# Fused cross attention and mixture of experts: all attention probabilities transposed by VectorE and regrouped through memory, with a fourth work bank

## The chip, the core and the metric

The kernel runs on one core of one Trainium2 chip. The metric is the device time of one execution in microseconds (us); lower is better. The core has five engines that work from their own instruction streams and meet at semaphores: TensorE (PE in the profile, its weight loads PEld), VectorE (DVE), ScalarE (ACT), GpSimd (POOL) and SyncE (SP, here the engine that issues nearly all DMA transfers).

## The reference

For 16 batches of 256 tokens of width 256, with a context of 256 tokens of width 192 for each batch:

```
q, k, v = layernorm(x) @ w_q, ctx @ w_k, ctx @ w_v        # 16 heads of 64
attn    = softmax(q @ k^T / 8)                            # per head, 256 x 256
x       = x + (attn @ v) @ w_o + b_o
g       = softmax(layernorm(x) @ router_w + router_b)     # 8 experts, top 2, capacity 640
x       = x + sum over the chosen experts of g * (gelu(h @ w1 + b1) @ w2 + b2)
```

## The kernel before

The kernel has two stages. The attention stage takes the first 700 us and is cut into 64 periods, four to a batch. Period m handles four heads (units 0 to 3) of 256 queries by 256 keys. The expert stage follows and is not touched by the change.

The order of the work is written out by hand. A function `timeline()` returns one list of (stage, number) pairs, and each engine walks that list and executes the stages that are its own. In period m (r is m modulo 4, the place in the batch) the engines do this:

- TensorE: `scores` of m (24 products into the PSUM banks 0 to 3, one bank a unit), `pv` of m-2 (probabilities times values), `q` and `k` of m+1 (projections), `v` of m, and between them the transposes `turn2` and `turn3` of m-1. In r=0 and r=2 comes a 24-product output projection `o`, in r=1 the transposes `xt` of the next batch, in r=2 and r=3 the router's `x2t` and `logits`.
- VectorE: four row maxima (`max0` to `max3`), `a_norm` of m-2 (the attended values times the inverse row sums, in place in PSUM), `inv`, `a_lo` of m-2, `q_lo`, `square0`, `k_lo`, `square1`, and then layer-norm and router work that differs with r.
- ScalarE: four exponentials `exp0` to `exp3` (two instructions each, with row sums), the copies `a_hi`, `q_hi`, `k_hi`, `v_sb` out of PSUM, and the copies of the two turned units (`copy2`, `copy3`).
- GpSimd: `ctx` (splits the next context), `ln1_root`, `ln2_root`, `residual`, and `scatter`, four indirect DMA writes a batch.
- SyncE: `inv_out` and `inv_in` (the inverse sums go through memory so that they come back spread over partitions), `lift` and `move`, and once a batch `traffic`.

The names with `_hi` and `_lo` are the two parts of a number: products of full precision are made of a rounded head and its remainder.

A probability tile must be transposed before it meets the values. That is done in two ways. In the 56 periods of `MOVED` (6 to 61), units 0 and 1 go through VectorE and memory: `square` transposes all 32x32 blocks in place, `lift` writes the tile to a table in memory, and `move` reads it back with the blocks in their turned places; `pv` two periods later uses it. Units 2 and 3 are transposed by TensorE into a PSUM bank (`turn`) and copied out by ScalarE. `by_pe(m)` says which units TensorE turns.

The results of `q`, `k`, `v`, `pv`, `xt`, `o`, `x2t` and `pos` share three PSUM banks (5 to 7) in rotation; each waits until the stage named in `WORK_READ` has read what was in the bank three works earlier. `logits` uses bank 4, which is the turns' bank.

Of the kernel before, what the change touches and what calls it, by code (L numbers as in the profile page):

```python
# [19 lines left out]
F32 = mybir.dt.float32  # L20
# [7 lines left out]
P = 128  # L28
B, S, D = 16, 256, 256
CD = 192  # L30
# [34 lines left out]
MOVED = range(6, PERIODS - 2)  # L65
SQ = 32
# [3 lines left out]
def by_pe(m):  # L70

    return (2, 3) if m in MOVED else (0, 1, 2, 3)

# [11 lines left out]
def timeline():  # L85
# [12 lines left out]
    for m in range(1, PERIODS - 2):  # L98
# [4 lines left out]
        out += [("scores", m)] + ([("pv", m - 2)] if m >= 2 else [])  # L103
        out += [("logits", b - 2)] if r == 3 and 2 <= b else []
# [16 lines left out]
        out += steps("exp0 exp1", m) + ([("a_hi", m - 2)] if m >= 2 else []) + [("q_hi", m + 1)]  # L121
        if four:
            out += [("copy0", m - 1), ("exp2", m), ("k_hi", m + 1), ("copy1", m - 1), ("exp3", m), ("copy2", m - 1),
                    ("v_sb", m)]
        else:
            out += [("copy2", m - 1), ("k_hi", m + 1), ("exp2", m), ("copy3", m - 1), ("exp3", m), ("v_sb", m)]
# [9 lines left out]
        out += ([("a_norm", m - 2)] if m >= 2 else []) + [("inv", m - 1)]  # L136
        out += [("slot", b - 3)] if r == 2 and 3 <= b else []
        out += [("bias", b - 2)] if r == 3 and 2 <= b else []
        out += [("ln1_stats", 1)] if m == 1 else []
        out += ([("a_lo", m - 2)] if m >= 2 else []) + [("q_lo", m + 1)]  # L140
        out += [("square0", m)] if m in MOVED else []
        out += [("k_lo", m + 1)]
        out += [("square1", m)] if m in MOVED else []
        if r == 0:
            out += steps("shift compare rank gate", b - 3) if 3 <= b else []
            out += [("ln1", b + 1)] if 1 <= b < B - 1 else []
# [3 lines left out]
        if r == 2:  # L150
# [11 lines left out]
                5: [("vsplit", 3)]}.get(m, [])  # L162
        out += [("scatter", b - 4)] if r == 0 and 4 <= b else []
# [5 lines left out]
        out += [("load_ctx", 3)] if m == 2 else []  # L169
        out += steps("inv_out inv_in", m - 1) + (steps("lift move", m) if m in MOVED else [])  # L170
# [1384 lines left out]
```

## Time and profile before

| | before |
|---|---|
| median of 3 runs | 955.09 us (954.37 to 957.1) |
| the profiled execution, own time | 957.82 us |
| its span, first to last instruction | 956.1 us |
| granted TensorE clock, mean | 0.992 of full |
| busy: PE | 918.1 us (96%) |
| busy: DVE | 739.8 us (77%) |
| busy: ACT | 573.8 us (60%) |
| busy: POOL | 280.2 us (29%) |

The span is the time from the first to the last instruction; the execution's own time is 1.7 us longer, and the median of the runs is 1.0 us below the span. Busy time is a sum of the stretches in which an engine has an instruction under way, so waits inside a stage do not count. The two stages have different limits, so the averages of the table say little about either.

### The profile page before, as it was taken

Reading aid. Unit: us, or ns where it says so; the run is one execution under the profiler, and the core shown is the slowest. Engines: PE = TensorE matmul, PEld = TensorE weight load, DVE = VectorE, ACT = ScalarE, POOL = GpSimd, SP = SyncE. Lnnn points to the kernel's source line nnn. Section 1 sums busy time; section 2 is a strip of 40 time slices with the busy share of each in tenths; the row PEclk is TensorE's granted clock in tenths of the full one; section 3 lists DMA queues with packets and bytes.
Section 4 is the critical chain, followed back from the end, with each engine's and each line's share of the span. In section 5 each row is a group of like instructions: output and inputs, shape, how many; then the busy total and the mean of one; then the engine's idle time right before and its main releaser. Section 6 shows DMA issues by size and latency. Waiting matters only on the chain.

```text
span 956.1 us, 22462 instructions
## 1 busy us (share of the span) xinstructions
PE 918.1 (96%) x7916; PEld 821.0 (86%) x7916; DVE 739.8 (77%) x1745; ACT 573.8 (60%) x1600; POOL 280.2 (29%) x441
## 2 busy tenths in 40 slices
PE   7999999999999999999999999999889999999995
PEld 7878888888888888888888888888689999999995
DVE  5757778888888888888888888877777877678762
ACT  5877766667667666766766677676534433334420
POOL 5541112314233231323223132302533223322233
PEclk9999999999999999999999999999899999999999
DMA  8462535445455445455444445444345765645422
GB/s 239 143 205 91 163 123 163 162 152 168 146 157 158 148 157 164 136 172 164 139 156 161 146 130 170 136 134 136 121 133 99 149 145 123 135 84 98 112 29 27
DMA packets 152991, 133.29 MB, mean 139 GB/s; under 512 B 62140, under 2 KB 141610, under 8 KB 152752
## 3 DMA queue, kind: packets, MB, share of 16 engines
q1 hardware_dynamic: 144048, 122.87, 42.9%
q0 software_dynamic: 8832, 8.98, 5.4%
q8 instruction: 64, 1.05, 0.5%
q14 instruction: 47, 0.39, 0.1%
HBM read 82.15 MB, written 54.61 MB: 143 GB/s over the span
## 4 chain that ended last, share of the span: by engine, by line
PE 70%; DVE 11%; ACT 10%; issue 4%; DMA 3%; POOL 0%; SPq 0%; POOLq 0%; ACTq 0%; DVEq 0%
PE psum L734 20%; PE psum L839 9%; PE psum L996 9%; PE psum L855 9%; PE psum L980 8%; PE psum L801 7%; ACT prob L1067 6%; PE psum L819 5%; DVE negmax L1255 3%; DVE hidl L1201 2%; DVE bufl L1201 1%; ACT probt L1007 1%; DVE hidh L1488 1%; PE psum L879 1%; DVE psum L1274 1%
## 5 line engine op out<-in xcount | busy, mean ns | idle before, releaser
L1067 ACT ACTIVATE prob<-psum,negmax 128x256 f32<-128x256 f32 x512 | 238.0, 481 | 79.5 <-DVE negmax L1255 79.4
L1255 DVE TENSOR_REDUCE negmax<-psum 128x2 f32<-128x512 f32 x256 | 160.4, 682 | 29.7 <-PE psum L801 29.7
L1173 ACT ACTIVATE hid<-psum,b1t 128x640 f32<-128x640 f32 x64 | 50.9, 795 | 126.6 <-PE psum L980 125.0
L839 PE MATMUL psum<-probt,v 128*64 128x256 f32 x1024 | 124.6, 385 | 0.0
L707 POOL DMA_INDIRECT out_rows<-y,rowi x40 | 66.3, 1658 | 160.8 <-DVE y L1498 154.2
L1067 ACT ACTIVATION_READ_ACCUMULATOR prob<-psum,negmax 128x1 f32 x512 | 109.5, 214 | 0.0
L839 PEld LDWEIGHTS psum<-probt,v 128*64 128x64 f32 x1024 | 67.8, 136 | 36.4 <-issue 0.3
L668 POOL DMA_INDIRECT slot_table<-row,picki x64 | 66.8, 1044 | 96.9 <-PE psum L734 61.2
L996 PE MATMUL psum<-w2h,hidh 128*128 128x256 f32 x320 | 91.4, 286 | 2.9 <-DVE y L1498 1.5
L801 PE MATMUL psum<-kh,qh 64*128 64x256 f32 x512 | 82.5, 316 | 11.1 <-ACT prob L1067 8.9
L996 PE MATMUL psum<-w2l,hidh 128*128 128x256 f32 x320 | 90.5, 283 | 0.0
L996 PE MATMUL psum<-w2h,hidl 128*128 128x256 f32 x320 | 90.5, 283 | 0.0
L1007 ACT ACTIVATE probt<-psum 128x512 f32<-128x512 f32 x144 | 87.3, 609 | 4.4 <-PE psum L819 4.4
L819 PE MATMUL psum<-ident,prob 128*128 128x128 f32 x576 | 87.1, 276 | 2.7 <-ACT prob L1067 2.7
L734 PE MATMUL psum<-xth,wqh 128*128 128x256 f32 x256 | 78.9, 308 | 0.5 <-DVE xtl L1201 0.5
L1279 DVE STREAM_TRANSPOSE prob<-prob 128x512 f32<-128x512 f32 x112 | 78.6, 702 | 0.0
L855 PE MATMUL psum<-woh,ah 128*128 128x256 f32 x256 | 72.9, 285 | 1.6 <-DVE al L1201 1.6
L606 POOL TENSOR_SCALAR shifted<-ln_mean_var 128x2 f32<-128x2 f32 x32 | 7.1, 223 | 225.0 <-issue 182.7
L801 PE MATMUL psum<-kl,qh 64*128 64x256 f32 x512 | 72.9, 278 | 0.0
L801 PEld LDWEIGHTS psum<-kh,qh 64*128 64x128 f32 x512 | 48.8, 185 | 27.9 <-ACT prob L1067 13.3
L801 PE MATMUL psum<-kh,ql 64*128 64x256 f32 x512 | 72.8, 277 | 0.0
L855 PE MATMUL psum<-wol,ah 128*128 128x256 f32 x256 | 72.4, 283 | 0.0
(199 smaller groups left out, 2704.6 us busy)
## 6 DMA issues: line engine op xcount, KB each, us to landing
squares<-prob SPq DMA_DIRECT2D x56, 512.0 KB
probt<-squares SPq DMA_DIRECT2D x224, 128.0 KB, 2.8
invrows<-inverses SPq DMA_DIRECT2D x128, 128.0 KB
w1r<-in_w SPq DMA_DIRECT2D x8, 1024.0 KB
w2r<-in_w SPq DMA_DIRECT2D x8, 1024.0 KB, 9.1
slot_table<-blank SPq DMA_DIRECT2D x8, 662.5 KB, 6.5
blocks<-slot_table SPq DMA_DIRECT2D x56, 80.0 KB
xin<-in_x SPq DMA_DIRECT2D x16, 256.0 KB, 3.5
```

Source lines behind the costliest of these rows:

```text
L668: pool.indirect_dma_start(out=table, out_offset=bass.IndirectOffsetOnAxis(ap=picki[:, b % 3, k, t:t + 1], axis=0), in_=row[:, b % 3, t, :] ...
L734: mm = pe.matmul(dst, lhs, rhs, start=(j == 0), stop=(j == len(terms) - 1))
L801: mm = pe.matmul(psum[:, 2 * cc + h, qb * S:(qb + 1) * S], a[r, m % 2, cc, cols], w[r, m % 2, cc, :], start=(j == 0), stop=(j == len(terms ...
L819: mm = pe.transpose(psum[:, TURN_BANK[u], kb * S + qb * P:kb * S + (qb + 1) * P], prob[:, m % 2, u, kb, qb, :], ident[:, :])
L839: mm = pe.matmul(dst[h * HD:(h + 1) * HD, cc * S:(cc + 1) * S], v[:, b % 2, kb, cols], p, start=(kb == 0), stop=(kb == ST - 1))
L855: mm = pe.matmul(dst[:, 0:D], a[:, b % 2, c, tt], w[:, c, :], start=(c == 0 and j == 0), stop=(c == PAIRS - 1 and j == 2))
L980: mm = pe.matmul(dst, lhs, rhs, start=(n == 0), stop=(n == len(terms) - 1))
L996: mm = pe.matmul(dst, a[:, j, ss], w[:, j, :], start=(j == 0 and m == 0), stop=(j == HC - 1 and m == 2))
L1007: copy = lambda dst, src, **kw: act.activation(dst, src, ACT.Copy, **kw)
L1067: last = act.activation(into, out_of, ACT.Exp, bias=negmax[:, m % 2, u, qb:qb + 1], accum_out=total[:, m % 2, u, qb:qb + 1])
L1255: dve.tensor_reduce(negmax[:, m % 2, u, :], psum[:, u, :].rearrange("p (q s) -> p q s", q=ST), AX.X, ALU.max, negate=True).then_inc(sem("m ...
L1279: dve.transpose(at, at).then_inc(sem("square"), 1)
```

## The change

All four units of a moved period now go through VectorE and memory, and TensorE turns none of them. Seven things change with that:

1. `turn2`, `turn3`, `copy2` and `copy3` are gone from the 56 periods. The layout of the moved tile covers four units: `square` handles two units in an instruction, `lift` and `move` carry twice the bytes in as many transfers, and `pv` reads all its probabilities in the moved layout.
2. `exp` of m waits for `lifted` of m-2 and no longer for `moved`.
3. TensorE's order in a period becomes `scores`, `logits` (in r=3), `q`, `k`, `pv`, `v`. ScalarE's becomes `exp0 exp1 q_hi exp2 k_hi exp3 a_hi v_sb`. VectorE's becomes `max0..3 inv q_lo square0 k_lo a_norm square1`.
4. Bank 4 joins the rotation of work banks (`places()`), and `logits` uses that rotation.
5. `a_norm` writes a new tile `attended` in SBUF, which frees its bank; `a_hi` reads that tile.
6. `a_lo` of the periods 4 to 59 and `ln1` of the batches from 2 on move from VectorE to GpSimd. `attended` is one tile, so `a_norm` of m waits for `a_lo` of m-1.
7. The context's raw tiles `c0` and `c1` have one buffer in place of two, `scatter` waits for `k` and no longer for `q`, and SyncE issues `lift` between `inv_out` and `inv_in`.

The core of the diff:

```diff
 def by_pe(m):
-    return (2, 3) if m in MOVED else (0, 1, 2, 3)
+    return () if m in MOVED else (0, 1, 2, 3)
...
         if four:
+            out += [("scores", m)] + ([("pv", m - 2)] if m >= 2 else [])
             out += [("q", m + 1), ("turn0", m - 1), ("k", m + 1), ("turn1", m - 1), ("v", m), ("turn2", m - 1)]
         else:
-            out += [("q", m + 1), ("turn2", m - 1), ("k", m + 1), ("turn3", m - 1), ("v", m)]
+            out += [("scores", m)] + ([("logits", b - 2)] if r == 3 and 2 <= b else [])
+            out += [("q", m + 1), ("k", m + 1), ("pv", m - 2), ("v", m)]
...
+        out += [("inv_out", m - 1)] + ([("lift", m)] if m in MOVED else [])
+        out += [("inv_in", m - 1)] + ([("move", m)] if m in MOVED else [])
...
-WORK_READ = {"xt": "xt_lo", "q": "q_lo", "k": "k_lo", "v": "v_sb", "pv": "a_lo", "o": "x2", "x2t": "x2t_sb",
+WORK_READ = {"xt": "xt_lo", "q": "q_lo", "k": "k_lo", "v": "v_sb", "pv": "a_norm", "o": "x2", "x2t": "x2t_sb",
...
+def places():
...
+    banks, last, found = [5, 6, 7], {}, {}
+    for stage, n in TIMELINE:
...
+        if work in WORKS and work not in found:
+            at = banks.pop(0)
+            banks.append(at)
+            found[work] = at, last.get(at)
+            last[at] = work
+        if (stage, n) == ("turn3", MOVED[0] - 1):
+            banks.append(4)
...
-                sp.dma_start(square_table[m % 2], prob_pair(m)).then_inc(sem("lifted"), 16)
+                sp.dma_start(square_table[m % 2], prob_all(m)).then_inc(sem("lifted"), 16)
...
-                at = work_bank("pv", m).rearrange("p (c s) -> p c s", c=2)
-                dve.tensor_tensor(at, at, invrows[:, :, :], ALU.mult).then_inc(sem("a_norm"), 1)
-
-            def square(m, u):
-                dve.wait_ge(sem("exp"), UNITS * m + u + 1)
-                at = prob_pair(m).rearrange("p (g u c) -> p u g c", g=GROUPS, u=2)[:, u]
+                if m >= 1:
+                    dve.wait_ge(sem("a_lo"), m)
+                dve.tensor_tensor(attended[:, :, :], work_bank("pv", m).rearrange("p (c s) -> p c s", c=2),
+                                  invrows[:, :, :], ALU.mult).then_inc(sem("a_norm"), 1)
+
+            def square(m, pair):
+
+                dve.wait_ge(sem("exp"), UNITS * m + 2 * pair + 2)
+                at = prob_all(m).rearrange("p (g v c) -> p v g c", g=GROUPS, v=2)[:, pair]
                 dve.transpose(at, at).then_inc(sem("square"), 1)
...
+            def a_lo(m):
+                b, c = divmod(2 * m, PAIRS)
+                pool.wait_ge(sem("a_hi"), m + 1)
```

VectorE in a period with r=3 of a middle batch, before: `al` is `a_lo`, `ql` and `kl` are `q_lo` and `k_lo`, and the two transposes of `prob` are `square0` and `square1`.

```order
L1255 TENSOR_REDUCE negmax<-psum 128x2 x4
L1274 TENSOR_TENSOR psum<-psum,invrows 128x512
L1264 RECIPROCAL invtot<-total 128x8
L1267 STREAM_TRANSPOSE invturned<-invtot 128x32
L1334 TENSOR_TENSOR logit<-psum,rb_all 128x16
L1201 TENSOR_TENSOR al<-psum,ah 128x512
L1244 SCALAR_TENSOR_TENSOR ql<-psum,qh 128x512
L1279 STREAM_TRANSPOSE prob<-prob 128x4x128
L1201 TENSOR_TENSOR kl<-psum,kh 128x512
L1279 STREAM_TRANSPOSE prob<-prob 128x4x128
```

The same period of the changed kernel:

```order
L1303 TENSOR_REDUCE negmax<-psum 128x2 x4
L1312 RECIPROCAL invtot<-total 128x8
L1315 STREAM_TRANSPOSE invturned<-invtot 128x32
L1384 TENSOR_TENSOR logit<-psum,rb_all 128x16
L1292 SCALAR_TENSOR_TENSOR ql<-psum,qh 128x512
L1330 STREAM_TRANSPOSE prob<-prob 128x4x256
L1249 TENSOR_TENSOR kl<-psum,kh 128x512
L1323 TENSOR_TENSOR attended<-psum,invrows 128x512
L1330 STREAM_TRANSPOSE prob<-prob 128x4x256
```

The transposes have doubled in width, `al` is gone, and the product with the inverse sums has moved from second place to just before the last transpose.

GpSimd in r=0 and r=1 of a middle batch, before: the context's split, the four scatters, the residual's bias, and the first instruction of `ln2_root`.

```order
L593 TENSOR_TENSOR c1s<-c,c1t 64x256
L594 TENSOR_TENSOR c0l<-c,c0h 128x256
L668 DMA slot_table<-row,picki 5120x265 x4
L631 TENSOR_TENSOR xin<-xin,bo_all 128x256 x2
L606 TENSOR_SCALAR shifted<-ln_mean_var 128x2
```

The same place of the changed kernel:

```order
L619 TENSOR_TENSOR c1s<-c,c1t 64x256
L620 TENSOR_TENSOR c0l<-c,c0h 128x256
L644 TENSOR_SCALAR turning<-xin,ln_mean_var,ln_rstd 128x256 x2
L713 DMA slot_table<-row,picki 5120x265 x4
L676 TENSOR_TENSOR xin<-xin,bo_all 128x256 x2
L655 TENSOR_TENSOR al<-attended,ah 128x512
L632 TENSOR_SCALAR shifted<-ln_mean_var 128x2
```

`ln1` stands ahead of the scatters and `a_lo` behind the residual, so this `a_lo` also waits for what those two wait for.

SyncE in r=1 and at the start of r=2 of a middle batch, before; the four transfers between the moves and the next `inverses` are `traffic` (the last row of it is two):

```order
L466 DMA inverses<-invturned 4x32x32
L475 DMA invrows<-inverses 64x2x256 x2
L485 DMA squares<-prob 128x1024
L492 DMA probt<-squares 32x4x256 x4
L404 DMA xin<-in_x 128x2x256
L500 DMA out_rows<-x 128x2x256
L411 DMA c<-in_ctxt 128x256
L413 DMA c<-in_ctxt 64x256 x2
L466 DMA inverses<-invturned 4x32x32
L475 DMA invrows<-inverses 64x2x256 x2
L485 DMA squares<-prob 128x1024
```

The same place of the changed kernel:

```order
L492 DMA inverses<-invturned 4x32x32
L511 DMA squares<-prob 128x2048
L501 DMA invrows<-inverses 64x2x256 x2
L518 DMA probt<-squares 32x4x512 x4
L433 DMA xin<-in_x 128x2x256
L526 DMA out_rows<-x 128x2x256
L440 DMA c<-in_ctxt 128x256
L442 DMA c<-in_ctxt 64x256 x2
L492 DMA inverses<-invturned 4x32x32
L511 DMA squares<-prob 128x2048
L501 DMA invrows<-inverses 64x2x256 x2
```

The lift to `squares` has doubled and stands ahead of the reload of the inverse sums.

## Rows read from the trace of the kernel before

**Rows 1.** Windows of two batches: length, then PE, PEld, DVE, ACT, POOL busy

```profile
215.59:257.63 42.04, 41.30 (x380) 35.57 (x379) 35.35 (x93) 29.12 (x92) 11.70 (x23) 1.00 0.52 160
425.79:467.83 42.04, 41.30 (x380) 35.57 (x379) 35.35 (x93) 29.11 (x93) 11.68 (x23) 1.00 0.48 155
```

**Rows 2.** Waits in the second batch: us in total, times, longest

```profile
DVE negmax L1255 <- PE psum L801: 1.2, 2, 0.9
...
DVE x L1297 <- PE psum L855: 0.3, 1, 0.3
...
PE psum L734 <- DVE valid L1382: 0.3, 1, 0.3
```

**Rows 3.** Chain of work in r=0 and r=1: start, us, what

```profile
430.10 1.64 PE psum L734 x12
431.74 0.44 PE psum L819 x4
432.18 1.19 PE psum L734 x10
...
437.82 1.62 PE psum L801 x24
439.44 1.88 PE psum L839 x16
```

**Rows 4.** Timeline of PE across one turn: start, us, engine, line

```profile
431.57 0.60 PE L819 MATMUL psum<-ident,prob 128*128 128x128 f32 x4
431.93 0.36 PE L734 MATMUL psum<-c0h,wkh 128*128 128x256 f32 x1
```

**Rows 5.** Groups of instructions by form: busy us, mean ns, idle before

```profile
L1279 DVE STREAM_TRANSPOSE prob<-prob 128x512 f32<-128x512 f32 x112 | 78.6, 702 | 0.0
...
L1201 DVE TENSOR_TENSOR al<-psum,ah 128x512 fp32r<-128x512 f32 x64 | 44.2, 691 | 19.1 <-ACT ah L1007 19.1
...
L1470 DVE STREAM_TRANSPOSE turned<-blocks 128x640 f32<-128x640 f32 x14 | 11.6, 834 | 0.0
...
L631 POOL TENSOR_TENSOR xin<-xin,bo_all 128x256 f32<-128x256 f32 x32 | 23.4, 730 | 52.9 <-DMA slot_table<-row,picki 30.2 <-DVE turning L1217 21.1 <-POOL ln_rstd L611 0.3
...
L622 POOL TENSOR_TENSOR w1l<-w1r,w1h 128x1024 fp32r<-128x1024 f32 x2 | 4.8, 2407 | 3.9 <-DMA slot_table<-row,picki 3.9
```

**Rows 6.** Timeline of DVE: r=3 ends, r=0 begins; `ln1` in r=0

```profile
425.53 0.70 DVE L1279 STREAM_TRANSPOSE prob<-prob 128x512 f32<-128x512 f32 x1
426.15 0.13 DVE L1431 TENSOR_REDUCE pick<-lowkey 128x2 f32<-128x16 f32 x1
...
427.30 2.47 DVE L1255 TENSOR_REDUCE negmax<-psum 128x2 f32<-128x512 f32 x4
...
437.74 0.74 DVE L1217 TENSOR_SCALAR turning<-xin,ln_mean_var,ln_rstd 128x256 f32<-128x256 f32 x2
```

**Rows 7.** Timeline of SP's DMA queue: start, us to issue, line, transfer

```profile
436.61 0.54 SPq L485 DMA_DIRECT2D squares<-prob  x1
440.34 1.82 SPq L492 DMA_DIRECT2D probt<-squares  x4
...
449.37 1.73 SPq L492 DMA_DIRECT2D probt<-squares  x4
...
453.87 0.58 SPq L466 DMA_DIRECT2D inverses<-invturned  x1
456.55 1.27 SPq L475 DMA_DIRECT2D invrows<-inverses  x2
```

**Rows 8.** The page's DMA issues: count, KB each, median us to landing

```profile
probt<-squares SPq DMA_DIRECT2D x224, 128.0 KB, 2.8
```

**Rows 9.** Timeline of POOL in r=0

```profile
426.02 0.39 POOL L590 CAST c1s<-c 64x256 fp32r<-64x256 f32 x1 [8.03 <-PE psum L734]
...
432.62 1.09 POOL L668 DMA_INDIRECT slot_table<-row,picki  x1 [3.63 <-PE psum L734]
...
440.59 1.54 POOL L631 TENSOR_TENSOR xin<-xin,bo_all 128x256 f32<-128x256 f32 x2 [2.95 <-DMA slot_table<-row,picki]
```

More of the change, by code:

```diff
@@ L118, in timeline @@
         out += [("pos", b - 3)] if r == 1 and 3 <= b else []
-        out += steps("exp0 exp1", m) + ([("a_hi", m - 2)] if m >= 2 else []) + [("q_hi", m + 1)]
         if four:
+            out += steps("exp0 exp1", m) + ([("a_hi", m - 2)] if m >= 2 else []) + [("q_hi", m + 1)]
             out += [("copy0", m - 1), ("exp2", m), ("k_hi", m + 1), ("copy1", m - 1), ("exp3", m), ("copy2", m - 1),
@@ L125, in timeline @@
         else:
-            out += [("copy2", m - 1), ("k_hi", m + 1), ("exp2", m), ("copy3", m - 1), ("exp3", m), ("v_sb", m)]
+            out += [*steps("exp0 exp1", m), ("q_hi", m + 1), ("exp2", m), ("k_hi", m + 1), ("exp3", m),
+                    ("a_hi", m - 2), ("v_sb", m)]
         if r == (1 if b else 2) and b + 1 < B:
@@ L135, in timeline @@
         out += ([("split_lo", 5)] if m == 1 else []) + steps("max2 max3", m)
[L136 to L142, printed above, removed]
+        if four:
+            out += ([("a_norm", m - 2)] if m >= 2 else []) + [("inv", m - 1)]
+            out += [("ln1_stats", 1)] if m == 1 else []
+            out += ([("a_lo", m - 2)] if 0 <= m - 2 < POOL_REST[0] else []) + [("q_lo", m + 1)]
+            out += [("square0", m)] if m in MOVED else []
+            out += [("k_lo", m + 1)]
+        else:
+            out += [("inv", m - 1)] + ([("slot", b - 3)] if r == 2 and 3 <= b else [])
+            out += [("bias", b - 2)] if r == 3 and 2 <= b else []
+            out += [("q_lo", m + 1), ("square0", m), ("k_lo", m + 1), ("a_norm", m - 2)]
         out += [("square1", m)] if m in MOVED else []
@@ L162, in timeline @@
                 5: [("vsplit", 3)]}.get(m, [])
+        out += [("ln1", b + 1)] if r == 0 and 1 <= b < B - 1 else []
         out += [("scatter", b - 4)] if r == 0 and 4 <= b else []
@@ L189, in timeline @@
             ("gelu_table", 0)]
-    out += [*steps("max0 max1 max2 max3", m), ("inv", m - 1), ("slot", c - 1), ("a_norm", m - 2), ("q_lo", z),
-            ("a_lo", m - 2), ("k_lo", z), ("ln2", c), *steps("keys pick", c - 1), ("x2add", ST * d), ("inv", m),
+    out += [*steps("max0 max1 max2 max3", m), ("inv", m - 1), ("slot", c - 1), ("q_lo", z), ("k_lo", z),
+            ("a_norm", m - 2), ("a_lo", m - 2), ("ln2", c), *steps("keys pick", c - 1), ("x2add", ST * d), ("inv", m),
             *steps("max0 max1 max2 max3", z), ("a_norm", m - 1), ("a_lo", m - 1), *steps("bias shift", c),
@@ L685, in _ @@
                     inverse_root(stage[:3], n)
+                if stage == "ln1" and n >= 2:
+                    ln1(n)
+                if stage == "a_lo" and n in POOL_REST:
+                    a_lo(n)
                 if stage == "vsplit":
@@ L844, in o @@
                 b, t = divmod(n, ST)
[L845 removed]
+                dst = bank("o", n) if chunks[0] == 0 else psum[:, PLACES["o", n][0], :]
                 tt = slice(t * P, (t + 1) * P)
@@ L1453, in _ @@
             for stage, n in TIMELINE:
-                if stage in steps:
+                if stage in steps and not (stage == "ln1" and n >= 2) and not (stage == "a_lo" and n in POOL_REST):
                     steps[stage](n)
```

127 lines of the change are left out of this document (70 added, 57 removed).

## The prediction

> **What bounds the kernel now.** I read the windows first. Two batches 210 us apart take 42.04 us each with the same busy times [rows 1], so the attention stage is a fixed cycle of one batch, four periods, and one batch can be priced and multiplied. In it PE is busy for 41.30 us, all but 0.74; the next column but one, DVE, has 35.35, ACT 29.1. The last columns say that the granted clock is full and that the 16 DMA engines are busy for about half of the time. So TensorE's own work sets the time of this stage. The waits say how far the second engine is from that. DVE has seven entries in the batch, from 1.2 us down to 0.3, in sum 5.8 us [rows 2]. What it does not wait is its own: 42.04 - 5.8 = 36.2 us, which is its 35.35 busy plus 0.9 of short gaps between instructions that depend on each other. The chain of work then confirms the bound: from r=0 into r=1 it runs through PE's steps one after another, 1.64 for `q`, 0.44 for a turn, 1.19 for `k`, later 1.62 for `scores` and 1.88 for `pv` [rows 3].
>
> **What the change takes from TensorE.** Eight turns a batch. The chain gives one 0.44 us [rows 3]. Start to start in the timeline it is 0.36 (431.57 to 431.93) [rows 4]; the rest is the slower first product behind it, which a change of operand may cost anyhow. I take the middle, 0.40. The 56 moved periods are 14 batches, so 112 turns x 0.40 = 44.8 us, with 40.3 and 49.3 as its ends. Besides, PE idles 0.74 us a batch. One of these waits is for `valid`, the reader of the `pos` bank, 0.3 us [rows 2]; with a fourth bank, and that reader now ahead of `q_lo`, it should go. I give half of the idle time back: 14 x 0.37 = 5.2 us. The sum is 50 us, with everything else hidden.
>
> **What it puts on VectorE.** Each of the two transposes grows from 512 to 1024 elements. The trace has 702 ns for 512 and 834 for 640, 1.03 ns an element [rows 5], so 1024 takes 1.23 us, 0.53 more. Per period that is +1.06. `a_lo` leaves: 0.69 of duration, but consecutive instructions of this kind start 0.62 apart (425.53 to 426.15) [rows 6], so -0.62. `ln1` leaves: 0.74 once a batch [rows 6]. The batch becomes 36.2 + 4 x 1.06 - 4 x 0.62 - 0.74 = 37.2 us. TensorE's becomes 42.04 - 3.2 - 0.4 = 38.4. So VectorE ends 1.2 us a batch under the new bound, 97% occupied, and its present 5.8 us of waits must shrink to 1.2. This is the step that I trust least. For it speaks the new order. Counted from the start of `scores`, the first bank is full at about 1.0; four maxima take 2.47 [rows 6], `inv` 0.4, and `q_lo` can start near 3.9. ScalarE has made two units and `q_hi` by about 4.1. Then come `square0` to 5.9, `k_lo` to 6.5, `a_norm`, whose `pv` ends at 1.62 + 1.64 + 1.19 + 1.88 = 6.3 [rows 3], and `square1` at 7.1, when `exp3` has ended near 6.5. Each product stands just behind its releaser, and `a_norm` no longer has `a_hi` and `a_lo` directly behind it. Batch work that is uneven over r (2.5 us of router work in r=0 where PE has an `o` of 24 products, little in r=3 where PE has none) falls in the same periods on both engines, so the lag between them stays within a microsecond. `exp3` must be done only when the second half of the next `scores` begins, some 3 us later; this is the play between the two.
>
> **ScalarE** loses two copies a period and was no bound. `a_hi` now reads SBUF, which may cost some tens of ns on an engine with 13 us of idle time a batch: nothing.
>
> **The trip through memory.** Lift before: issued at 436.61, its data landed when `move` is issued at 440.34: 3.7 us for 512 KB [rows 7]. The moves took 1.82 to issue and 2.8 to land [rows 7, 8], some 4.6. If size cost nothing the trip stays 8.3 us; if all doubles it is 16.6. Between these ends I take, as an estimate, that half of each step grows with the bytes: 12.5 us. `square1` ends about 8.3 us after its period's `scores`; `pv` stands two periods later, behind `scores`, `q` and `k` (4.45). With a period of 9.6 us the trip may take 2 x 9.6 + 4.45 - 8.3 = 15.3 us. So it is hidden with 2.8 us to spare, and in the worst case late by 1.3.
>
> SyncE's queue is the tighter place. In r=1 it issues the moves at 449.37 and, behind `traffic`, the next `inverses` only at 453.87 and the reload `invrows` at 456.55 [rows 7]. After the change the lift stands ahead of that reload and takes 1 to 2 us more, so the reload lands about 8 to 9 us behind `square1` of r=2. Its reader is `a_norm` in the next period (r=3), about 8 us behind that `square1`: a wait of 0 to 1 us, once a batch.
>
> **GpSimd.** `a_lo` is 512 elements wide: 730 ns for 256 and 2407 for 1024 give 2.18 ns an element [rows 5], so 1.29 us. In r=0 it stands behind the scatters. The first scatter started 0.9 us behind the end of `q` and now follows `k`, 1.19 later; the four take until 5.0 us later, the residual waited 2.95 more and took 1.54 [rows 3, 9]. From the start of r=0: 1.62 + 1.64 + 1.19 + 0.9 + 5.0 + 2.95 + 1.54 + 1.3 = 16.1 us. r=0 lasts about 10.5, so `attended` comes free 5.6 us into r=1, and `a_norm` there wants it at about 6.5. It holds by 0.9 us. A scatter that lands 2 us later on busier DMA engines costs VectorE 1 us a batch. These two places are why I give back only half of PE's idle time.
>
> There is a price that could sink the change: GpSimd now reads and writes SBUF for 1.3 us more a period. In the trace a 512-wide transpose (425.53 to 426.23) has a GpSimd cast from SBUF starting at 426.02 inside it; both keep their usual 702 and 390 ns [rows 5, 6, 9]. So I price this contention at nothing; the other end is that VectorE stands still for each `a_lo`, 1.29 us a period. The Trainium skill speaks against the change here. Its page "SBUF — State Buffer", section "SBUF: two separate sides", says that VectorE and GpSimd share a port pair as an exclusive lock, which a VectorE operation in a two-port mode or with two SBUF inputs takes for its whole length. Read strictly it covers here the router's comparisons and the layer norm, not the transposes, if these run in one-port mode; by that rule the sum moves by a microsecond or two at most.
>
> **Sum.** Profiled: span 956.1 - 50 = 906, own time 957.8 - 50 = 908. The median of the runs shown is 2.7 us under that profiled execution, so 905.
>
> **Rivals.**
>
> *VectorE takes over.* For it: two engines near 97% in a loop rarely both run free, and VectorE waits seven times a batch even now, with 14% of its time to spare. Against it: the order above. If half of the 5.8 us stays, the batch is 37.2 + 2.9 = 40.1 us, and the gain 14 x 1.9 = 27: 928. If all stays, 43.0 and 14 us slower. Chance of something between 913 and 952: 0.22.
>
> *GpSimd blocks VectorE* (ends slower). If every `a_lo` stops VectorE for 1.29 us, VectorE's batch is 37.2 + 5.2 = 42.4 and with 1.2 us of waits 43.6: 955 + 14 x 1.5 = 977. It decides from about 0.9 us of blocking a period on. Against it stands the overlap above: 0.05. The skill's rule, were the transposes two-port operations, is this case.
>
> *The trip is late.* It becomes slower than before only when the trip exceeds 2 x 10.5 + 4.45 - 8.3 = 17.2 us, above even the doubled 16.6. At 16.6 the period settles where 2p - 3.85 = 16.6, p = 10.2: gain 14 x 1.2 = 17, 938. Chance 0.05.
>
> *It saves more.* Turns at 0.44 and all of PE's idle time gone: 49.3 + 10.4 = 60 us, 895. Chance of under 897: 0.08.
>
> **How the numbers follow.** The forecast, TensorE still the bound and 897 to 913, has 0.58; what is left, 0.02, is the change doing nothing. The range for 8 in 10 leaves out the low case and the slow end: 896 to 930 takes all of the forecast and most of the first rival. About 0.3% (3 us) is what a measurement of this kernel can tell from no change; faster by more 0.91, within it 0.03, slower 0.06 (the blocking case and the far end of the first rival).
>
> **What would show it.** Right: a batch of 38 to 38.8 us; PE busy for over 97% of it with no `ident,prob` products; VectorE near 96%; transposes of 1.23 us; GpSimd's `al` near 1.29. The rivals would show as `scores` waiting for `prob` while DVE is full, as transposes longer than 1.3 us while GpSimd works, as `pv` waiting for the DMA of `squares`, or as `attended` waiting for `al` (r=1) or `invrows` (r=3).

## The result and the profile after

| | before | after |
|---|---|---|
| median | 955.42 us (954.37 to 957.1, 4 runs) | 985.12 us (982.63 to 987.04, 4 runs) |
| span of the profiled execution | 956.1 us | 980.9 us |
| mean granted clock | 0.992 | 0.983 |

The ratio is 1.031, 95% interval 1.028 to 1.034. The forecast was 905 us. The changed kernel is 30 us slower than before, 80 from the forecast. Further down, one run each of e16 (1001.25 us) and e19 (952.10 us) was slow, over 1.5% above the fastest of its kernel, and the medians given here leave it out.

First the page of the changed kernel: section 1, the DMA rows of section 2 (40 slices, each digit the busy share in tenths), the chain, and the issues with their time to landing.

```profile
PE 887.5 (90%) x7468; PEld 780.1 (80%) x7468; DVE 749.3 (76%) x1661; ACT 513.0 (52%) x1488; POOL 386.9 (39%) x525
...
DMA  8465888888887888888879887887543855545422
GB/s 232 134 207 172 241 259 232 243 241 260 238 242 230 232 257 247 226 243 261 238 225 251 253 241 230 234 258 210 161 148 78 168 127 128 108 79 129 110 28 27
...
DMA 28%; PE 24%; POOL 17%; DVE 12%; issue 11%; ACT 4%; SPq 4%; POOLq 0%; DVEq 0%; ACTq 0%
...
squares<-prob SPq DMA_DIRECT2D x56, 1024.0 KB, 6.1
probt<-squares SPq DMA_DIRECT2D x224, 256.0 KB, 5.0
...
xin<-in_x SPq DMA_DIRECT2D x16, 256.0 KB, 6.1
```

The chain that ended last runs for 28% of the span through transfers, more than through TensorE. PE has lost 30.6 us of work (918.1 to 887.5), and yet the span grew by 24.8. A move that landed 2.8 us after its issue [rows 8] now takes 5.0. The load of `xin`, which the change does not touch, takes 6.1.

Two windows, the steady stretch and one batch, with columns as in [rows 1]. The last two are the busy share of the DMA engines and GB/s.

```profile
127.39:653.03 525.64, 469.60 (x4125) 391.29 (x4122) 431.20 (x1021) 296.72 (x997) 224.94 (x339) 0.99 0.84 242
394.08:437.62 43.54, 38.82 (x349) 32.56 (x345) 35.99 (x87) 24.71 (x84) 19.23 (x29) 1.00 0.87 245
```

The batch takes 43.54 us where 38 to 38.8 was forecast, and 42.04 before. PE's work is 38.82 us, down from 41.30 (the prediction's terms give 41.30 - 3.2 = 38.1), so the turns are saved. But 4.7 us of the batch are now idle on PE. The busy share of the DMA engines, 0.52 and 0.48 in the two batches of [rows 1], is 0.87. VectorE has 35.99 us of work, and its waits in this batch fill nearly all of the rest, 36.0 + 7.2 = 43.2 of 43.54:

```profile
DVE stats L1256 <- DMA xin<-in_x: 3.6, 1, 3.6
DVE attended L1323 <- POOL al L655: 2.5, 1, 2.5
DVE ql L1292 <- ACT qh L1054: 1.1, 4, 0.3
```

Two places hold VectorE for 6.1 us in this batch. Both stand behind transfers. First r=2, on SyncE's queue and on VectorE's timeline:

```profile
424.55 1.73 SPq L518 DMA_DIRECT2D probt<-squares  x4
426.69 0.40 SPq L433 DMA_DIRECT2D xin<-in_x  x1
...
432.46 0.76 DVE L1256 BATCH_NORM_STATS2 stats<-xin 128x6 f32<-128x256 f32 x2 [3.60 <-DMA xin<-in_x]
```

The load goes out directly behind 1 MB of moves and takes 5.8 us, while VectorE stands in front of it with everything else of r=2 queued behind. Then r=0 on GpSimd (compare [rows 9]), and what VectorE waits for in r=1:

```profile
445.68 2.44 POOL L644 TENSOR_SCALAR turning<-xin,ln_mean_var,ln_rstd 128x256 f32<-128x256 f32 x2
448.30 1.12 POOL L713 DMA_INDIRECT slot_table<-row,picki  x1 [0.18 <-POOL turning L644]
...
457.86 1.54 POOL L676 TENSOR_TENSOR xin<-xin,bo_all 128x256 f32<-128x256 f32 x2 [4.54 <-DMA slot_table<-row,picki]
459.49 1.28 POOL L655 TENSOR_TENSOR al<-attended,ah 128x512 fp32r<-128x512 f32 x1
...
460.89 0.69 DVE L1323 TENSOR_TENSOR attended<-psum,invrows 128x512 f32<-128x512 f32 x1 [1.25 <-POOL al L655]
```

`ln1` (2.44 us) stands ahead of the scatters, the residual waits 4.54 us for them in place of 2.95, and the remainder ends at 460.8. VectorE's wait for it is 1.25 us here and 2.5 in the batch above.

### The profile page after: what moved, and what is told of

The parts are those of the page before. It is cut to its first block, busy times and chain, and to the rows that moved or that the text cites. A ratio compares the mean times of both kernels' runs of the same rounds, so it can differ in the third digit from the quotient of the medians.

```text
span 980.9 us, 21255 instructions
## 1 busy us (share of the span) xinstructions
PE 887.5 (90%) x7468; PEld 780.1 (80%) x7468; DVE 749.3 (76%) x1661; ACT 513.0 (52%) x1488; POOL 386.9 (39%) x525
## 4 chain that ended last, share of the span: by engine, by line
DMA 28%; PE 24%; POOL 17%; DVE 12%; issue 11%; ACT 4%; SPq 4%; POOLq 0%; DVEq 0%; ACTq 0%
DMA squares<-prob 9%; PE psum L1043 9%; PE psum L1027 8%; DMA xin<-in_x 7%; DMA slot_table<-row,picki 7%; POOL al L655 4%; POOL slot_table L713 4%; SPq L518 3%; DVE prob L1330 3%; DMA inverses<-invturned 2%; PE psum L779 2%; POOL turning L644 2%; POOL xin L676 2%; ACT prob L1115 2%; DVE hidl L1249 2%
## 5 line engine op out<-in xcount | busy, mean ns | idle before, releaser
L1115 ACT ACTIVATE prob<-psum,negmax 128x256 f32<-128x256 f32 x512 | 241.3, 492 | 161.6 <-DVE negmax L1303 157.2
L886 PE MATMUL psum<-probt,v 128*64 128x256 f32 x1024 | 129.4, 396 | 12.6 <-DMA probt<-squares 12.4
L1330 DVE STREAM_TRANSPOSE prob<-prob 128x1024 f32<-128x1024 f32 x112 | 137.9, 1232 | 0.7 <-ACT prob L1115 0.7
L1115 ACT ACTIVATION_READ_ACCUMULATOR prob<-psum,negmax 128x1 f32 x512 | 114.8, 224 | 0.0
L886 PEld LDWEIGHTS psum<-probt,v 128*64 128x64 f32 x1024 | 74.2, 141 | 48.8 <-issue 21.3
L655 POOL TENSOR_TENSOR al<-attended,ah 128x512 fp32r<-128x512 f32 x56 | 71.6, 1279 | 72.6 <-ACT ah L1054 69.4
L846 PE MATMUL psum<-kh,qh 64*128 64x256 f32 x512 | 80.4, 304 | 11.6 <-issue 7.2
L1054 ACT ACTIVATE ah<-attended 128x512 fp32r<-128x512 f32 x64 | 40.5, 633 | 87.2 <-DVE attended L1323 87.2
L1323 DVE TENSOR_TENSOR attended<-psum,invrows 128x512 f32<-128x512 f32 x64 | 43.6, 682 | 40.4 <-POOL al L655 28.2
```

The lines of the kernel that those rows point to most:

```text
L655: pool.tensor_tensor(al[:, b % 2, c:c + 2, :], attended[:, :, :], ah[:, b % 2, c:c + 2, :].bitcast(F32), ALU.subtract).then_inc(sem("a_lo" ...
L846: mm = pe.matmul(psum[:, 2 * cc + h, qb * S:(qb + 1) * S], a[r, m % 2, cc, cols], w[r, m % 2, cc, :], start=(j == 0), stop=(j == len(terms ...
L886: mm = pe.matmul(dst[h * HD:(h + 1) * HD, cc * S:(cc + 1) * S], v[:, b % 2, kb, cols], p, start=(kb == 0), stop=(kb == ST - 1))
L1115: last = act.activation(into, out_of, ACT.Exp, bias=negmax[:, m % 2, u, qb:qb + 1], accum_out=total[:, m % 2, u, qb:qb + 1])
L1330: dve.transpose(at, at).then_inc(sem("square"), 1)
```

## The experiments

Medians over 3 rounds each (5 for e18 and e19), against runs of the kernel before on the same chip, which gave 955.9 (e1 to e4), 956.4 (e6 to e9), 958.8 (e10 to e12), 958.7 (e13 to e16) and 958.1 (e17 to e19). There is no e5. The stretch 130 to 600 us is used for windows and waits unless another is named.

The expectations name their theories by letters. A: the doubled traffic makes transfers late, and two of them stop VectorE. B: the new order of the stages and VectorE's load set the time. C: GpSimd blocks VectorE. D: SyncE's queue, which issues and waits one step after another, sets the time. E: the rate of the 16 DMA engines sets it. H: a move that writes 32 partitions is slow and the order of such moves matters. W: the scattered write into SBUF is slow, and not the 32 partitions.

**Are the two waits the loss?** e1 moves the statistics of the layer norm and their root from r=2 to r=3, e2 puts GpSimd's remainder ahead of the residual in r=0, e3 does both.

```diff
-            out += [("ln1_stats", b + 2)] if b + 2 < B else []
+        out += [("ln1_stats", b + 2)] if r == 3 and b + 2 < B else []
...
+        out += [("a_lo", m - 2)] if r == 0 and m - 2 in POOL_REST else []
         out += [("residual", b + 1)] if r == 0 and 1 <= b < B - 1 else []
```

> The changed kernel with one edit: the first layer norm's statistics of batch b+2 and their root are moved from r=2 to the end of r=3, some 10 us behind the load that they read. In the changed kernel VectorE waits 3.6 to 4.9 us a batch there for the transfer of xin. Theory A (the doubled traffic makes single transfers late, and two of them stop VectorE): this wait goes and the batch falls by 2.5 to 4 us over some 13 batches, so 985 becomes 935 to 952; the wait of attended for al in r=1 stays at about 2.3 us a batch. Rival B (the new order of the steps and VectorE's load set the time, and the wait only fills slack): the time that VectorE waited for xin comes back as other waits, result 975 to 988. Rival C (GpSimd blocks VectorE through the shared memory port): no change beyond 5 us.

> The changed kernel with one edit: in r=0 GpSimd's a_lo stands between the scatters and the residual, so it no longer waits for the scatters' transfers to land. Theory A: the 2.3 us a batch that attended waits for al in r=1 go; since r=1 leads to the late load in r=2, whose time is set by SyncE's queue and not by VectorE, part of it comes back there: 955 to 975. Rival B: 980 to 988. Rival C (port): no change.

> Both edits together. Theory A: both waits go, the batch comes to 38.5 to 40 us, and the kernel to 915 to 930, below the kernel before (955). Rival B: it stays above 955. Rival C: GpSimd's blocking stays in, so 945 or more, with transposes and scalar operations of VectorE longer than in the kernel before while al runs.

Measured: e1 987.29 (ratio 1.032, 1.030 to 1.034), e2 988.32 (1.034, 1.033 to 1.036), e3 980.21 (1.026, 1.024 to 1.028). Each cured wait is gone from its trace and comes back elsewhere. In e1 `attended` waits 35.9 us for `al` where the changed kernel has 26.5 in the same stretch; in e2 the wait for `xin` is 45.1 where it was 39.2. With both gone, 5 of the 80 us are back, where theory A expected 915 to 930. So the two waits are not the loss; they are where VectorE met it first. Theories B and C still stand after these three runs. In e3 it is PE that waits for the moves (8.6 us in this stretch of the changed kernel):

```profile
PE psum L887 <- DMA probt<-squares: 30.9, 17, 3.0
```

SyncE's own queue waits in e3 (127 to 653 us, as engine line waited for: total, times, longest):

```profile
SPq L502 <- DMA inverses<-invturned: 169.5, 48, 4.7
SPq L519 <- DMA squares<-prob: 73.4, 49, 2.8
```

So a 16 KB transfer that was handed over right behind 1 MB of moves holds SyncE's queue 3.5 us a period.

**The bytes.** e4 lifts and moves only the first half of each block row (the other half of the probabilities that `pv` reads is old). e8 lifts all and moves half.

```diff
-                sp.dma_start(square_table[m % 2], prob_all(m)).then_inc(sem("lifted"), 16)
+                sp.dma_start(square_table[m % 2].rearrange("p (g c) -> p g c", g=GROUPS),
+                             prob_all(m).rearrange("p (g c) -> p g c", g=GROUPS)[:, :, 0:256]).then_inc(sem("lifted"), 16)
```

> The changed kernel, with lift and move carrying half of each tile (256 of every 512 columns, 512 KB a step as in the kernel before); the attention output is built in part from old probabilities. Instructions and order on the five engines are those of the changed kernel. Theory A: DMA share falls from 0.85 to about 0.5 and the transfers land about as before, xin's wait falls below 1 us and al's below 0.5 us a batch: 905 to 925, near what was predicted. Rivals B and C: the bytes don't matter, 970 to 988.

> The changed kernel with only the moves cut to half the bytes (256 of every 512 columns; the rest of a tile keeps what it had, so the attention output is not the reference's); the lift carries all 1024 KB. With both halved the kernel takes 911. Moves fill the DMA engines for 4 to 5 us a period at 235 GB/s, the lift for 2.6 at 400. Theory E: most of the loss is with the moves, 920 to 935. Theory D: the loop loses only the moves' part ahead of inverses, and a similar 915 to 940. If the lift's size was the cost, 955 to 980.

Measured: e4 911.26 (0.953, 0.952 to 0.955), e8 922.67 (0.965, 0.962 to 0.968). With the bytes of before, all other parts of the change give what was forecast, to within 6.3 us, which rules out B and C as the main cause: order, engines and GpSimd's work are those of the changed kernel. Of the 74 us between e4 and the changed kernel, 62 go with the second half of the moves and then 11 with that of the lift. The two windows (e4, then e8) have 165 and 216 GB/s:

```profile
130.00:600.00 470.00, 463.31 (x4178) 388.88 (x4177) 436.61 (x1036) 302.37 (x1010) 226.79 (x337) 1.00 0.56 165
```

```profile
130.00:600.00 470.00, 454.99 (x4101) 381.57 (x4101) 427.25 (x1017) 294.31 (x989) 222.68 (x334) 1.00 0.65 216
```

One batch of e4 has TensorE busy from end to end, in 38.8 us as forecast; the eleven loads of `xin` in the stretch are 38.8 us apart in the mean too:

```profile
413.50:452.30 38.80, 38.80 (x353) 32.62 (x353) 36.70 (x90) 25.67 (x86) 19.79 (x30) 1.00 0.56 169
```

A kernel with the lift alone halved was not tried.

**Traffic without the change.** e9 is the kernel before with two copies of 512 KB from the table to spare memory behind the moves of each period.

```diff
+                for h in range(2):
+                    sp.dma_start(spare[m % 2, h], square_table[m % 2]).then_inc(sem(f"moved{m % 2}"), 16)
```

> The kernel before, unchanged in its order and its engines' work, with two more copies of 512 KB from memory to memory behind each period's four moves (from the table of squares to a spare table), which pv and the next exponentials wait for with the moves. That is as much added traffic as the change adds. If the traffic alone costs the time (theories D and E), the kernel before slows down too: 985 to 1040, with VectorE waiting for xin or PE for the moves. If the loss needs the change's order of steps on the engines (theory B), it stays within 955 to 965.

Measured 1125.54 (1.176, 1.170 to 1.181), the worst miss of the expectations. The copies share the moves' counter, so `pv` waits for them too (58.7 us in the stretch), and the granted clock of the stretch fell from 1.00 to 0.93; the size is not a price of traffic alone. What can be read are the waits for transfers that the edit did not touch. Before, this stretch had 2.5 us of waits for `invrows` and 1.1 for `xin`:

```profile
DVE psum L1277 <- DMA invrows<-inverses: 71.9, 28, 4.6
DVE stats L1211 <- DMA xin<-in_x: 40.5, 9, 6.2
```

**SyncE's order.** e6 is e3 with the move of m-1 ahead of `inv_in`, and the lift behind it, so that no wait for `inverses` holds the lift. e7 is e6 with the four moves issued for partition groups 0, 2, 1, 3.

```diff
-        out += [("inv_out", m - 1)] + ([("lift", m)] if m in MOVED else [])
-        out += [("inv_in", m - 1)] + ([("move", m)] if m in MOVED else [])
+        out += [("inv_out", m - 1)] + ([("move", m - 1)] if m - 1 in MOVED else [])
+        out += [("inv_in", m - 1)] + ([("lift", m)] if m in MOVED else [])
...
-                for g in range(GROUPS):
+                for g in (0, 2, 1, 3):
```

> Both edits of the third experiment, and SyncE's order changed: a period now issues inv_out of m-1, move of m-1, inv_in of m-1, lift of m, traffic. So the small write of the inverse sums no longer queues behind the four moves, and its reload no longer behind a lift. In the third experiment SyncE spent 3.5 us a period waiting for the landing of inverses and 1.5 for the lift, one after the other, in a loop of about 10 us. Theory D (the serial loop of SyncE's queue sets the period, not the bytes): the wait for inverses goes, the loop has slack, the batch comes to 38 to 39.5 us and the kernel to 905 to 930. Theory E (the 16 DMA engines' bandwidth sets the period; they are busy for 86% and each transfer only waits for others): the DMA share rises to above 0.93 at most, the batch falls by no more than 3 us of 43, 945 to 975.

> The kernel e6_order, with the four moves issued for the partition groups 0, 2, 1, 3 in place of 0, 1, 2, 3. Each move writes 32 of 128 partitions and the trace shows 16 busy DMA engines moving only about 235 GB/s while moves run, against 400 or more in a lift. If neighbouring moves share a part of the memory's ports, alternating halves raises the rate of the moves and takes 5 to 20 us from e6_order under theory E, less than 5 under theory D. If the rate comes from reading 2 KB pieces, no change within 3 us.

Measured: e6 990.13 (1.035, 1.033 to 1.038), e7 975.68 (1.021, 1.018 to 1.024). In e6 the wait for `inverses` is gone (2.3 us where e3 has it at every period) but the moves go out later, `pv` waits 45.2 us for them, and the kernel is 10 us slower than e3. Both expectations missed (D 905 to 930, E 945 to 975). This order of the queue gains nothing; that a part of the loss is SyncE's serial order is not ruled out by it. e7 gained 14.5 us with nothing but the order of four equal DMAs, within the 5 to 20 expected.

**The shape of the DMAs.** All on the base of e3, all with the same bytes. e10 is e3 with the order 0, 2, 1, 3. e11 issues groups 0 and 1 from SyncE and 2 and 3 from ScalarE. e12 lets the lift do the regrouping, so that the move is one DMA over 128 partitions. e13 and e14 leave the regrouping out (`pv` reads probabilities in the wrong places): one move of 128 partitions, and four moves of 32 in which each partition takes one run of 8 KB. A tile of 1 MB over 128 partitions is 8 KB in each, so a regrouping move takes four runs of 2 KB; the expectations of e13 and e14 have both at half their size.

```diff
e12
-                sp.dma_start(square_table[m % 2], prob_all(m)).then_inc(sem("lifted"), 16)
+                for a in (0, 2, 1, 3):
+                    sp.dma_start(square_table[m % 2].rearrange("(g j) (a c) -> a j g c", a=GROUPS, g=GROUPS)[a],
+                                 prob_all(m)[a * SQ:(a + 1) * SQ, :].rearrange("j (g c) -> j g c", g=GROUPS))\
+                      .then_inc(sem("lifted"), 16)
...
e12 and e13, in place of the four moves
+                sp.dma_start(probt_all(m), square_table[m % 2]).then_inc(sem(f"moved{m % 2}"), 16)
e14
+                    sp.dma_start(probt_all(m)[g * SQ:(g + 1) * SQ, :], square_table[m % 2][g * SQ:(g + 1) * SQ, :])\
```

> e3 (both waits cured) with one thing changed: the four moves of a period are issued for partition groups 0, 2, 1, 3 in place of 0, 1, 2, 3. Same bytes, same number of DMAs, same order of everything else. Theory H (a move of 32 partitions reaches only some of the ports of SBUF, and neighbouring groups share them, so that the order decides how well two moves in flight overlap): some 10 to 16 us below e3's 980, as the same edit brought 14.5 us on another base, so 964 to 970, with a higher rate of the DMA engines. Rival (bytes alone set the period, and the gain on the other base was one of order): 977 to 983.

> e3 with moves of groups 0 and 1 issued from SyncE's queue and those of groups 2 and 3 from ScalarE's queue, so that both halves are written at the same time and SyncE issues two DMAs a period less. Theory H: as e10 or better, 955 to 970. Rival that the queue of SyncE is the bound (its issues one behind another): better than e10 too, with SyncE's wait for the inverses gone. Rival that bytes alone set the period: 977 to 983. If ScalarE's wait for the lift holds up its exponentials: above 985, with ScalarE waiting for the DMA of squares.

> e3 with the regrouping done on the way out: four lifts of 32 partitions each write the table in the layout of the destination, and one move of 1 MB over all 128 partitions brings it back. Same bytes, same number of DMAs a period. Theory H (a DMA over 32 partitions is the slow part, wherever it stands): the lift becomes slow, the move fast; the sum changes little, 970 to 985, unless writes into SBUF are slower than reads from it. Theory W (it is the scattered write into SBUF that is slow, not the 32 partitions): 925 to 955, the DMA share down towards 0.7.

> e3 with the regrouping left out altogether: one lift of 1 MB and one move of 1 MB, both over 128 partitions and in one piece of 4 KB a partition, so that the value products read probabilities in the wrong places; the bytes are the same as in e3, a period has two DMAs less than e12's five. Theory W/H (the shape of the DMAs costs, not the bytes): at or below e12's 945, 915 to 935, the DMA share at 0.75 or lower, since e4 with half of the bytes took 911. Rival (bytes alone): 970 to 980.

> e3 with four moves over 32 partitions each as there, but each partition takes one run of 4 KB in place of four of 1 KB (again no regrouping, the value products read probabilities in the wrong places). If the 32 partitions are what slows a move, it stays near e3: 970 to 985. If the runs of 1 KB do it, it comes near e13: 915 to 940.

| | move | us | less the kernel before | ratio | DMA share | GB/s |
|---|---|---|---|---|---|---|
| e3 | 4 x 32 partitions, 2 KB runs | 980.21 | +24.3 | 1.024 to 1.028 | 0.86 | 245 |
| e10 | the same, order 0, 2, 1, 3 | 969.64 | +10.8 | 1.007 to 1.013 | 0.84 | 248 |
| e14 | 4 x 32 partitions, 8 KB runs | 958.04 | -0.7 | 0.997 to 1.002 | 0.88 | 254 |
| e11 | as e3, from two queues | 956.51 | -2.3 | 0.995 to 1.001 | 0.84 | 255 |
| e12 | 1 x 128, the lift regroups | 945.10 | -13.7 | 0.982 to 0.993 | 0.82 | 262 |
| e13 | 1 x 128, no regrouping | 932.91 | -25.8 | 0.971 to 0.976 | 0.78 | 267 |

The windows of e3, e14 and e13 in this order:

```profile
130.00:600.00 470.00, 423.62 (x3700) 355.76 (x3696) 395.15 (x929) 267.75 (x894) 207.05 (x315) 0.97 0.86 245
```

```profile
130.00:600.00 470.00, 435.12 (x3851) 364.19 (x3852) 407.79 (x957) 279.32 (x933) 212.78 (x328) 0.99 0.88 254
```

```profile
130.00:600.00 470.00, 452.64 (x4071) 378.17 (x4070) 428.80 (x1011) 295.42 (x980) 225.59 (x342) 1.00 0.78 267
```

e13 moves more bytes a second at a lower busy share than e3. The busy share counts the time that the engines hold a packet, not what they carry.

The kernel before ran 3 us slower beside e10 to e14 than beside e3, so the differences to it are the safer measure. By them the 50 us between e3 and e13 (47 in the times) split into 25 (22) for the runs of 2 KB in place of 8 KB (e3 to e14) and 25 for four DMAs of 32 partitions in place of one of 128 (e14 to e13). e14 fell between its two expectations for that reason: both things cost. The second step changes two things at once, the partitions that a DMA reaches and the number of DMAs, which these runs do not part.

e10 shows that the order matters by itself (13.5 us), since it changes neither the number nor the bytes. e12 bears out W rather than H alone: its four lifts are of 32 partitions and in runs of 2 KB too, and yet it is 38 us faster than e3. But the shape acts on SyncE's queue as well: its wait for `inverses`, 151.8 us in e3 in this stretch, is 40.7 in e13 and 3.4 in e12. And the bytes themselves cost: e13, of the cheapest shape, is still about 20 us above e4.

The Trainium skill, page "SBUF — State Buffer", section "Door 1: The DMA port swizzle (why [64,N] ≈ [32,N])", says that partitions 0 to 63 are reached through one half of the 16 DMA ports and 64 to 127 through the other, so that groups 0 and 1 use the same half and 2 and 3 the other. The gains of e7 and e10 fit that mapping, but no trace here shows a port, so it is a reading and not a shown cause. e11 does not decide it: two queues also halve the time in which SyncE issues moves (1.73 us for four in the changed kernel), though SyncE still waits 123.4 us for `inverses` there.

**The order of the stages, with the cheaper shape.** e15 is the changed kernel with e12's lift and move and neither stage of e3 moved; e16 has the statistics moved, e17 the remainder. e18 is e15 with the remainder of one period in four, the one due in r=0, back on VectorE behind `square1`; e19 is e18 with the statistics in r=3.

```diff
+def on_pool(m):
+    return m in POOL_REST and m % PER_B != 2
...
+        out += [("a_lo", m - 2)] if m - 2 in POOL_REST and not on_pool(m - 2) else []
```

> The changed kernel with the regrouping done by the lift, as e12, but without e3's two moves of stages. With less trouble in the DMA engines the two moves of stages may be worth nothing: e12's trace has VectorE's row operation (128 x 256) at 0.75 us against 0.42 elsewhere, since GpSimd's al now runs beside it. 935 to 945 if that costs more than the waits they cure; 950 to 960 if the waits for xin and al come back.

> e15 with only the statistics of the layer norm moved to r=3 (the load of xin gets one more period). If e15 waits for xin: 5 to 15 us better than e15, 930 to 942. If not: within 3 us of it.

> e15 (the lift regroups) with only GpSimd's remainder put ahead of the residual in r=0. e15 waits 31 us for xin and 10 for al, e12 with both moves of stages takes 945, e16 with the statistics alone 990. If the late remainder is what e16 shows (al waits 48 us there) and the wait for xin is worth some 20 to 30 us by itself, this run keeps the wait for xin and loses the one for al: 945 to 955. If curing one of the two waits always feeds the other, as with e1 and e2: above 960.

> e15 with the remainder of the period that ends in r=0 back on VectorE, behind square1: GpSimd's queue behind the scatters then holds none of the remainders, at 0.62 us a batch for VectorE. If the lateness of that remainder is what is left of the loss: 930 to 945, with VectorE's waits for al gone, those for xin staying (some 30 us in 470). Rival (VectorE is now the bound, at 90% busy): 950 to 960.

> e18 with the statistics of the layer norm in r=3 as well, so that neither the load of xin nor a remainder stands behind a late transfer. If these two waits and the shape of the moves were the whole of the loss beside the bytes: at or below e12's 945, 925 to 940, near e13's 933. If the waits return elsewhere, as in e16: above 960.

Measured: e15 955.33 (0.995 to 0.998), e16 988.84 (1.026 to 1.031), e17 957.18 (0.998 to 1.001), e18 948.64 (0.987 to 0.993), e19 939.69 (0.978 to 0.983). e17 fell between its two expectations, and so did e18, in which the waits for `al` are gone and those for `xin` stay at 30.2 us. e16 is the miss to learn from: with the wait for `xin` cured alone it is 34 us slower than e15. GpSimd's queue gets the root of the layer norm in r=3, where it waits for VectorE's statistics, and holds a remainder and all of r=0's work behind it (GpSimd's timeline in e16):

```profile
441.83 0.23 POOL L632 TENSOR_SCALAR shifted<-ln_mean_var 128x2 f32<-128x2 f32 x1 [12.08 <-DVE ln_mean_var L1259]
...
444.03 1.28 POOL L655 TENSOR_TENSOR al<-attended,ah 128x512 fp32r<-128x512 f32 x1
```

In r=1 the late remainder then holds VectorE, and VectorE holds TensorE (e16's waits):

```profile
DVE attended L1323 <- POOL al L655: 48.2, 10, 7.6
...
PE psum L779 <- DVE attended L1323: 34.7, 10, 6.4
```

With r=0's remainder out of GpSimd's queue the same edit gains 9 us (e18 to e19). e19 is 2.0% faster than the kernel before (0.980, 0.978 to 0.983), the best that computes the whole. Its window, and the longest waits left of DVE, PE and ACT's exponentials:

```profile
130.00:600.00 470.00, 447.16 (x3973) 373.85 (x3972) 426.97 (x999) 287.52 (x955) 205.63 (x322) 0.99 0.82 260
```

```profile
DVE ql L1300 <- ACT qh L1062: 17.5, 35, 2.8
...
PE psum L926 <- DVE row L1273: 17.2, 11, 2.6
...
ACT prob L1123 <- DMA squares<-prob: 48.8, 19, 3.0
```

PE and VectorE hardly wait for a transfer any more, but ScalarE does: `exp` waits for the lift that empties its tile, 48.8 us in the stretch, the longest of these waits, and VectorE's wait for `qh` stands behind ScalarE. A third buffer for `prob` was not tried.

**TensorE's clock.** A part of the loss that the waits do not name is the granted clock. In the changed kernel PE is busy for 0.09 of the 2 us from 300 to 302, and from 304 to 306 it works at 0.50, the lower of its two levels (1.2 of 2.4 GHz), with 12 products done where 27 are done from 308 to 310:

```profile
300.00:302.00 2.00, 0.09 (x2) 0.07 (x1) 1.90 (x12) 0.00 (x0) 0.95 (x2) 1.00 0.79 321
...
304.00:306.00 2.00, 2.00 (x12) 1.11 (x10) 1.68 (x6) 2.00 (x8) 0.39 (x1) 0.50 0.66 155
```

Added up over slices of 5 us of the stretch, the clock that was not granted comes to 0 us in the kernel before, e4, e8 and e13, to 5.1 in the changed kernel, 3.4 in e14 and e15, 12.0 in e3, 17.4 in e16 and 20.4 in e6 (in the profiled execution of each). As an estimate, that is the most it can have cost where PE was the bound: up to 14 of the 34 us between e15 and e16, and up to 12 of the 50 between e3 and e13. So a wait of PE can cost here twice, once as idle time and once as clock.

## Why the prediction was wrong

**What bounds the kernel, the turns, VectorE's work: right.** The PE work of a batch is 38.82 us (38.1 by the prediction's terms, which had the batch at 38.4); the transpose of 1024 elements takes 1.23 us and `al` on GpSimd 1.28, as forecast:

```profile
L1330 DVE STREAM_TRANSPOSE prob<-prob 128x1024 f32<-128x1024 f32 x96 | 118.2, 1231 | 0.0
...
L655 POOL TENSOR_TENSOR al<-attended,ah 128x512 fp32r<-128x512 f32 x49 | 62.6, 1278 | 57.5 <-ACT ah L1054 54.7 <-POOL ln_rstd L637 0.2
```

e4 confirms the sum as a whole: 911 where it gave 905, and a batch of 38.8 us. The contention of GpSimd and VectorE, which the sum priced at nothing, was not quite nothing: in the changed kernel a `pick` of each batch takes 749 ns in place of 169, 5.8 us of VectorE's time in the stretch of 470, where the prediction spoke of a microsecond or two by the rule that it named.

**The trip through memory: the step that failed.** It asked one main question of the doubled transfers, whether the trip still fits between `square1` and `pv` ("So it is hidden with 2.8 us to spare"), and the answer was nearly right. Its trip was 12.5 us; by the same steps one trip of the changed kernel takes 11.8 (lift issued at 419.53, moves at 424.55, 1.73 to issue, 5.0 to land), and `pv` waits 9.0 us in twelve batches, 0.75 each. What it priced at nothing, but for a microsecond at the scatters and one at `invrows`, is what 2 MB more a batch of lifts and 2 MB more of moves do to all other transfers on the same engines. Their busy share of 0.5 stood in [rows 1]; doubled traffic takes it to 0.87, and a load of 256 KB that landed in 3.5 us takes 6.1. VectorE's wait for `xin`, 3.6 us in the batch above, is in no term of the sum. It is the first sign of the missing term and not its size: e1 removes the wait and gains nothing. e4 against the changed kernel sizes the whole, direct and through other stages and the clock, at 74 us. How the 74 us divide between the rate of the DMA engines, SyncE's queue and the clock stays open.

**GpSimd in r=0: wrong for two reasons.** From the start of r=0 to the end of the remainder the prediction had 16.1 us. It took 20.6, from the first product of `scores` in PE's timeline to the end of `al` at 460.8:

```profile
440.13 0.39 PE L846 MATMUL psum<-kh,qh 64*128 64x256 f32 x2 [0.85 <-issue]
```

`ln1` was taken off VectorE's sum and never put on this one. By the steps of [rows 3], `k` ends 4.45 us behind that start, at 444.6, and the first scatter starts 3.7 us behind it and not 0.9. The landing of the scatters took 1.6 us more. "A scatter that lands 2 us later on busier DMA engines costs VectorE 1 us a batch" was about right for its part. The wait is 28.2 us in the twelve batches, in eleven of them. In e4, where only the missing `ln1` is left, VectorE waits for `al` 10.3 us in the stretch of 470, in ten of its batches.

**The reload of `invrows`: smaller than allowed.** No wait of VectorE for it appears in the twelve batches; four waits of `a_norm`, 3.5 us together, have no releaser in the trace.

**The rivals.** "VectorE takes over" came true in form, but its waits were not those of two close engines: they ended on transfers, and `attended` waiting for `al` in r=1 was a sign that the prediction had named. "The trip is late" named the right resource and the wrong reader. "GpSimd blocks VectorE" was right to be small: the transposes keep 1.23 us. None had a case in which transfers that the change doesn't touch come late and make the kernel slower, so the chance of slower, 0.06, was too low.

## What to carry to other kernels

When a change adds bytes, list every transfer that shares the engines and ask how late each reader can bear it; the busy share did not tell whose transfer would be late. Here the regrouping of 32-partition blocks through memory was better done on the way out, with one full-width DMA back: 35 us (e3 to e12, 38 against the kernel before of the same runs) for no byte less. Cure waits in pairs with the queue that they feed; one alone can cost more than it gives (e16).

## What the runs showed of the hardware

Four DMAs of 32 partitions in the order 0, 2, 1, 3 are faster than in the order 0, 1, 2, 3, by 14.5 us over 56 periods (e6 to e7) and 13.5 (e3 to e10, each against the kernel before of its own runs; 10.6 in the times), about 0.25 us a period.

Some VectorE operations of the form TENSOR_SCALAR take longer when GpSimd works beside them. In the changed kernel this one starts at 441.94, when `al` runs on GpSimd from 441.37 to 442.66, and takes 0.75 us where the kernel before has 0.17:

```profile
441.94 0.75 DVE L1483 TENSOR_SCALAR pick<-pick 128x2 f32<-128x2 f32 x1
```

In e19, where GpSimd's stages fall elsewhere, `pick` is back at 170 ns and it is `row` that pays, 747 ns in the mean against 391, 8 us in the stretch (the mean mixes two: the median is 408 ns, the longest 1116):

```profile
L1273 DVE TENSOR_SCALAR row<-x,ln_mean_var,ln_rstd 128x256 f32<-128x256 f32 x22 | 15.6, 747 | 0.0
```

The transposes never grow: 1221 to 1245 ns for all 112, also for one that starts at 447.20 while GpSimd's `ln1` runs from 445.68 to 448.12. The Trainium skill's page "SBUF — State Buffer", section "SBUF: two separate sides", which the prediction set beside it, describes an exclusive lock between VectorE and GpSimd; the traces agree for TENSOR_SCALAR and show none of it for STREAM_TRANSPOSE.
